# The last shared-expert step moved behind the routed experts, next to the closing layernorm

## The chip, the cores and the metric

The kernel runs on one core of a Trainium2 chip. It is one launch that computes two sequence-mixing layers and two feed-forward layers in f32. The metric is the device time of that launch in microseconds (us), taken as the median of several runs. A profile is one further execution, recorded by the hardware profiler. TensorE is called PE in its rows, VectorE DVE, ScalarE ACT, GpSimd POOL and SyncE SP. "PEld" is the weight load that goes with a matmul.

## The reference, cut to what matters

Only the last feed-forward layer and the layernorm around it are touched. Its input x has 4 sequences of 1024 rows with 256 columns each. The attention layers ahead of it are not changed.

```python
def _ffn(x, w1, w2, w3):
    return jax.nn.silu(x @ w1.T) * (x @ w3.T) @ w2.T

shared = jnp.zeros_like(xf)
for i in range(sw1.shape[0]):              # 2 shared experts, every row
    shared = shared + _ffn(xf, sw1[i], sw2[i], sw3[i])
logits = xf @ router_w.T + expert_bias     # 8 routed experts
rw, sel = jax.lax.top_k(logits, TOPK)      # each row goes to 2 of them
rw = jax.nn.softmax(rw)
...                                        # out = sum over the chosen experts of rw * _ffn
out = out + shared
x = _layernorm(x + out)                    # over the 256 columns
```

## The kernel before

Each of the three last phases is a block of its own: all engines meet at its end before the next one begins. Every f32 operand of a matmul is split into a high part in a shorter format (`fp32r`) and a low remainder, and each product is three matmuls (`PARTS`). The hidden size is 512, so one expert is `HM` = 4 hidden tiles of 128.

`phase_shared` works the two shared experts over 8 steps (`STEPS`) of 512 rows (`TOK`). A step is `NM` = 8 turns, one for each hidden tile of both experts. In turn m PE computes the two "up" products (12 matmuls of 512 columns), ACT takes `Silu` of one, DVE multiplies it by the other (`g`), ACT copies the high part (`ghi`), DVE subtracts to get the low part (`glo`), and PE adds the "down" product of turn m-2 (12 matmuls of 256 columns) into PSUM banks 6 and 7. `output(i)` on DVE adds the residual rows and SP stores the sum to the DRAM tensor `xs`. SP also reloads rows (`xr`) and fills the table `wall` with the weights of the 8 routed experts (`load_expert`). The first step also makes the router's logits, the second the routing. Then POOL scatters all rows by expert into the DRAM tensor `xg` with indirect DMAs (L1878).

`phase_experts` works 39 groups (`GROUPS`) of 256 gathered rows. The buffer `whl` has two slots that alternate: the high weights are cast out of `wall` by DVE, ACT and POOL, the low ones come by DMA from `wlo` (`up_low`, `down_low` on SP). PE runs the up products at L2384 (12 of 256 columns in a turn, four turns in a group), the transposes of the next group's rows at L2349, and the down products at L2364. ACT scales the result (`output`, L2311) and POOL adds it into `xs` by indirect DMA (`add_rows`, L2280), one group after the other. The small DMA `paid` (L2251) brings 16-byte pieces for all slots.

`phase_combine` is the closing layernorm of all 4096 rows, in 8 chunks of 512 consecutive rows: load from `xs` by SP and ACT (L2487, L2505), statistics on DVE (L2524), a chain of small operations in 16 columns that ends in the reciprocal square root (L2528 to L2536 and the helper `rsqrt`, L84 to L89), then scaling on ACT (L2501) and DVE (L2544) and the store to `out`. Statistics and chain are done for 4 chunks, then for the other 4.

The order of work on an engine is the order in which the code is written, and semaphores tie the engines together. `in_pairs` and `in_turns` run a body for pairs of steps with a hardware loop in the middle. A step touches rows c*128 to c*128+127 of each sequence, whereas a chunk of the closing layernorm is 512 consecutive rows of one sequence, so the last step's rows lie in the last quarter of every second chunk.

## Time and profile before

| | us |
|---|---|
| runs: median (lowest to highest of 3) | 1491.15 (1490.99 to 1496.67) |
| profiled execution, its own time | 1489.9 |
| profiled execution, span of the trace | 1488.3 |
| shared experts' 8 steps, from the first product to the last, by the trace | 782 to 1083 |
| routed experts' 39 groups | 1092.7 to 1444.8 |
| closing layernorm, first load to the end | 1457.7 to 1488.3 |

The span runs from the first to the last instruction. Busy shares over it are 92% for PE, 61% for DVE, 46% for ACT and 36% for POOL. In rows of the timeline the first number is the start and the second the duration, "x12" counts merged instructions, and square brackets hold the idle time of the engine just ahead and what ended it. Where rows are merged the duration runs from the first one's start to the last one's end.

### The profile page before, as it was taken

The page shows a single profiled execution, that of the slowest core. Times are in us where ns is not written, and L with a number is a line of the kernel's source. Part 1 is how long each engine was busy: PE and PEld are TensorE (multiplying, and loading weights), DVE is VectorE, ACT ScalarE, POOL GpSimd, SP SyncE. Part 2 cuts the span into 40 slices and gives each one's busy share as a digit, 9 for nine tenths or more (in the row PEclk, how much of TensorE's full clock was granted, in tenths as well). Part 3 has the DMA queues.
Part 4 walks back from the last instruction along what each step waited for, and adds up shares of the span by engine and source line. Part 5 has one row for each costly group of instructions (what it writes and reads, how often), then busy time and mean ns, then how long its engine had stood idle before and what let it go on. Part 6 is the DMA issues. An engine that isn't in the chain of part 4 may idle for free. (4 is left out here: it accounts for less than half of the span.)

```text
span 1488.3 us, 34037 instructions
## 1 busy us (share of the span) xinstructions
PE 1369.8 (92%) x12248; PEld 1189.6 (80%) x12248; DVE 906.9 (61%) x1924; ACT 687.1 (46%) x1260; POOL 540.9 (36%) x490
## 2 busy tenths in 40 slices
PE   6889999979999999999978999999979999999980
PEld 5778888867777777777757888888869999999980
DVE  4757676678687777787763364444345555555545
ACT  2446765544544544544533232222235555555543
POOL 0235554452345445445110025522014444444440
PEclk7799999979999999999998999999989999999995
DMA  6333442022213323312126014242178888888866
GB/s 237 118 130 108 145 153 85 30 86 105 86 58 127 116 67 127 120 63 99 61 69 257 19 51 149 96 149 68 54 198 237 230 238 233 233 244 235 230 144 229
DMA packets 101066, 204.00 MB, mean 137 GB/s; under 512 B 18433, under 2 KB 72577, under 8 KB 94721
## 3 DMA queue, kind: packets, MB, share of 16 engines
q1 hardware_dynamic: 75888, 144.66, 30.3%
q0 software_dynamic: 23088, 54.31, 12.8%
q10 hardware_dynamic: 2016, 4.08, 0.7%
q8 instruction: 44, 0.72, 0.2%
q14 instruction: 30, 0.24, 0.0%
HBM read 144.46 MB, written 58.55 MB: 136 GB/s over the span
## 5 line engine op out<-in xcount | busy, mean ns | idle before, releaser
L2384 PE MATMUL ps<-e_xhl,e_whl 128*128 128x256 f32 x1872 | 248.2, 282 | 5.1 <-DMA e_whl<-wlo 5.1
L2384 PEld LDWEIGHTS ps<-e_xhl,e_whl 128*128 128x128 f32 x1872 | 233.0, 189 | 5.6 <-issue 5.6
L1958 PE MATMUL ps<-s_xhl,s_whl 128*128 128x512 f32 x768 | 192.6, 400 | 6.1 <-PEq L1079 6.1
L1958 PEld LDWEIGHTS ps<-s_xhl,s_whl 128*128 128x128 f32 x768 | 143.8, 193 | 35.3 <-issue 6.3
L2280 POOL DMA_INDIRECT xs<-e_y,e_slot_id x78 | 121.8, 1561 | 83.1 <-ACT e_y L2311 68.5
L463 POOL TENSOR_TENSOR b_hhl<-b_h,b_hhl 128x512 fp32r<-128x512 f32 x64 | 94.5, 1479 | 139.6 <-ACT b_hhl L727 118.1
L2364 PE MATMUL ps<-e_whl,e_ghl 128*128 128x256 f32 x936 | 137.7, 282 | 0.5 <-DVE e_ghl L2458 0.5
L2446 DVE TENSOR_TENSOR e_g<-ps,e_act_h 128x256 f32<-128x256 f32 x156 | 66.2, 425 | 115.8 <-ACT e_act_h L2325 115.8
L2364 PEld LDWEIGHTS ps<-e_whl,e_ghl 128*128 128x128 f32 x936 | 120.5, 188 | 0.7 <-ACT e_ghl L2335 0.7
L2138 DVE TENSOR_TENSOR d_g<-ps,d_act_h 128x512 f32<-128x512 f32 x64 | 44.2, 691 | 124.4 <-PE ps L1958 87.4
L2325 ACT ACTIVATE e_act_h<-ps 128x256 f32<-128x256 f32 x156 | 60.0, 385 | 111.4 <-PE ps L2384 111.4
L560 PE MATMUL ps<-b_w,b_hhl 128*128 128x256 f32 x768 | 105.3, 287 | 6.2 <-DVE b_turned_rows L833 5.4
L560 PEld LDWEIGHTS ps<-b_w,b_hhl 128*128 128x128 f32 x768 | 99.2, 192 | 11.5 <-issue 5.8
L1937 PEld LDWEIGHTS ps<-s_whl,d_ghl 128*128 128x128 f32 x768 | 101.2, 192 | 4.8
L1937 PE MATMUL ps<-s_whl,d_ghl 128*128 128x256 f32 x768 | 104.5, 287 | 0.0
L547 PE MATMUL ps<-b_xhl,b_w 128*128 128x512 f32 x384 | 104.2, 406 | 0.1
L2273 POOL CAST e_whl<-wall 128x1024 fp32r x39 | 40.5, 1039 | 165.7 <-PE ps L2364 118.1
L1476 ACT ACTIVATE c_qf<-c_cf,fc 128x512 f32<-128x512 f32 x64 | 46.2, 722 | 117.8 <-DVE c_cf L1607 117.8
L1258 POOL TENSOR_TENSOR c_elo<-c_eraw,c_ehi 128x1024 fp32r<-128x1024 f32 x24 | 57.2, 2382 | 107.2 <-ACT c_ehi L1493 99.4
L2458 DVE TENSOR_TENSOR e_ghl<-e_g,e_ghl 128x256 fp32r<-128x256 f32 x156 | 66.1, 424 | 41.2 <-ACT e_ghl L2335 41.0
L1607 DVE TENSOR_SCALAR c_cf<-ps,fc 128x1024 f32<-128x1024 f32 x64 | 85.6, 1337 | 4.8 <-PE ps L1390 4.4
L2002 ACT ACTIVATE d_ghl<-d_g 128x512 fp32r<-128x512 f32 x64 | 40.4, 632 | 100.9 <-DVE d_g L2138 98.7
(356 smaller groups left out, 2654.4 us busy)
## 6 DMA issues: line engine op xcount, KB each, us to landing
e_whl<-wlo SPq DMA_DIRECT2D x39, 1024.0 KB, 5.1
e_whl<-wlo SPq DMA_DIRECT2D x39, 512.0 KB, 3.8
c_eraw<-in_expert_w POOLq DMA_DIRECT2D x24, 512.0 KB, 4.9
wlo<-c_elo POOLq DMA_DIRECT2D x24, 512.0 KB, 3.0
wall<-in_expert_w SPq DMA_DIRECT2D x8, 1536.0 KB, 8.5
xg<-b_zeros POOLq DMA_DIRECT2D x13, 780.0 KB, 3.8
e_xr<-xg SPq DMA_DIRECT2D x39, 260.0 KB, 3.9
x<-rows_out SPq DMA_DIRECT2D x16, 512.0 KB, 3.2
```

Source lines behind the costliest of these rows:

```text
L463: gp.tensor_tensor(hhl[:, m % 4, 1], h[:, m % 4], hhl[:, m % 4, 0].bitcast(F32), ALU.subtract).then_inc(s["hlo_ready"], 1)
L547: mm = pe.matmul(ps[:, H + m % 2, :], w1s[:, wp, kd, m * P:(m + 1) * P], xhl[:, k, xp, kd, :], start=q == 0, stop=q == 3 * KD - 1)
L560: mm = pe.matmul(ps[:, O + b // 2, lo:lo + D], hhl[:, m % 4, hp, b * P:(b + 1) * P], w2s[:, wp, m, :], start=m == 0 and q == 0 and b % 2 = ...
L1607: ve.tensor_scalar(cf[:, u % 2], ps[:, FB:FB + 2, :], fc[:, HIGH], fc[:, LOW], ALU.min, ALU.max).then_inc(s["clip_done"], 1)
L1937: mm = pe.matmul(ps[:, O + b // 2, (b % 2) * D:(b % 2 + 1) * D], ghl[:, m % 4, gp_, b * P:(b + 1) * P], whl[:, wp_, m // HM, lo:lo + D], s ...
L1958: mm = pe.matmul(ps[:, H + 2 * (m % 2) + w, :], whl[:, wp, e, lo:lo + P], xhl[:, k, xp, kd, :], start=q == 0, stop=q == 3 * KD - 1)
L2280: gp.indirect_dma_start(xs, bass.IndirectOffsetOnAxis(ap=slot_id[:, i, b:b + 1], axis=0), y[:, k, b, :], None, compute_op=ALU.add).then_in ...
L2325: act.activation(act_h[:, m], ps[:, H + m, 0:SLOT], ACT.Silu).then_inc(s["silu_done"], 1)
L2364: mm = pe.matmul(ps[:, O + k, b * D:(b + 1) * D], ghl[:, m, gp_, b * P:(b + 1) * P], whl[:, k, wp_, lo:lo + D], start=m == 0 and q == 0 an ...
L2384: mm = pe.matmul(ps[:, H + m, w * SLOT:(w + 1) * SLOT], whl[:, k, wp, lo:lo + P], xhl[:, k, xp, kd, :], start=q == 0, stop=q == 3 * KD - 1)
L2446: ve.tensor_tensor(g[:, m], ps[:, H + m, SLOT:2 * SLOT], act_h[:, m], ALU.mult).then_inc(s["g_ready"], 1)
L2458: ve.tensor_tensor(ghl[:, m, 1], g[:, m], ghl[:, m, 0].bitcast(F32), ALU.subtract).then_inc(s["glo_ready"], 1)
```

## The change

The shared phase now does 7 steps (`LAST = STEPS - 1`). Step 7's rows go into `xs` as they are (SP stores them from `xr`), so that the routed experts' additions land on them. In step 2 SP writes the split shared weights from SBUF to a new DRAM tensor `shared_hl` (6 MB in two DMAs), and waits for them before the phase ends.

In the experts' block SP loads the last step's rows (`rows7`) at the start. After the last group PE, ACT and DVE work the last shared step there (`turn7`, `up7`, `down7`, `high7`, `low7`), with the weights brought back from `shared_hl` into the two slots of `whl`. `phase_combine` is gone: its 8 chunks are loaded by SP once all scattered additions have landed, DVE makes their statistics between the turns of the last shared step (`STATS_AT`), ACT scales chunks 0, 1, 2, 4, 5 and POOL chunks 3, 6, 7. The rows of step 7 in the odd chunks are left out of the stores (96 of 128 partitions); they are finished on their own by DVE at the end, from the shared sum in PSUM plus their rows of `xs` (`x7`).

```diff
@@ phase_shared, SP
-            for i in range(STEPS):
+            for i in range(LAST):
...
+                if i == 2:
+                    for e in range(SHARED):
+                        sp.dma_start(shared_hl[:, e], whl[:, :, e].bitcast(F32)).then_inc(s["kept_out"], 16)
...
                 if i == 5:
-                    sp.wait_ge(s["xlo_ready"], STEPS)
+                    sp.wait_ge(s["xlo_ready"], LAST)
                     load_expert(5)
+            sp.wait_ge(x_in[LAST % 2], 16 * (LAST // 2 + 1))
+            sp.dma_start(xs[LAST], xr[:, LAST % 2, :, 0:D]).then_inc(s["stored"], 16)
+            sp.wait_ge(s["kept_out"], 16 * SHARED)
@@ phase_shared, PE (ACT and DVE alike)
-            in_pairs(pe, PAIR, body)
+            in_turns(pe, LAST, body)
@@ phase_experts, SP
+            sp.dma_start(rows7[:], last_x3).then_inc(f["rows7_in"], 16)
...
+            def shared_weights(n):
+                k = SLOT_OF[n]
+                sp.wait_ge(s["h_done"], HM * (GROUPS - 1 + n))
+                sp.dma_start(whl[:, k, :, 0:W2AT].bitcast(F32), shared_hl[:, n, :, 0:W2AT]).then_inc(shared_up_in[n], 16)
+                sp.wait_ge(s["g_used"], HM * (GROUPS - 1 + n))
+                sp.dma_start(whl[:, k, :, W2AT:WCOLS].bitcast(F32), shared_hl[:, n, :, W2AT:WCOLS]).then_inc(shared_down_in[n], 16)
...
+            sp.wait_ge(scattered, 16 * SB * GROUPS)
+            for i in range(STEPS):
+                sp.dma_start(x[:, bb(i)], xs_rows[i]).then_inc(rows_in[i], 16)
+            sp.dma_start(x7[:], last_xs).then_inc(f["x7_in"], 16)
@@ phase_experts, POOL, behind the last scatter
+            for i in GP_ROWS:
+                gp.wait_ge(f["scales_ready"], 1 + i // HALF)
+                for b in range(BATCH):
+                    t = i * BATCH + b
+                    last = gp.tensor_scalar(o[:, t, :], x[:, t, :], small[:, 3, t:t + 1], small[:, 5, t:t + 1], ALU.mult, ALU.add)
+                last.then_inc(f["by_gp"], 1)
@@ phase_experts, ACT
+            for m in range(NM):
...
+                act.activation(act7[:, m % 2], ps[:, H + 2 * (m % 2), :], ACT.Silu).then_inc(f["silu7_done"], 1)
...
+                act.activation(ghl7[:, m % 4, 0], g7[:, m % 2], ACT.Copy).then_inc(f["ghi7_ready"], 1)
+                if m == 0:
+                    act.wait_ge(scattered, 16 * SB * (GROUPS - 2))
+                    output(GROUPS - 1, (GROUPS - 1) % 2)
+                if m >= 6:
+                    normalise(ACT_ROWS[m - 6])
+            for i in ACT_ROWS[2:]:
+                normalise(i)
@@ phase_experts, PE
+                    if m == 1 and is_turn(j, k, GROUPS - 1):
+                        turn7()
...
+            pe.wait_ge(f["xhi7"], 1)
+            pe.wait_ge(f["xlo7"], 1)
+            for m in range(NM):
+                up7(m)
+                if m == 0:
+                    for m_ in (2, 3):
+                        down(GROUPS - 1, (GROUPS - 1) % 2, m_, (GROUPS - 1) // 2)
+                if m >= 2:
+                    down7(m - 2)
+            for m in range(NM - 2, NM):
+                down7(m)
@@ phase_experts, DVE
+            STATS_AT = {3: (0,), 4: (1, 2), 5: (3,), 6: (4, 5), 7: (6, 7)}
...
+            for m in range(NM):
...
+                ve.tensor_tensor(g7[:, m % 2], ps[:, H + 2 * (m % 2) + 1, :], act7[:, m % 2], ALU.mult).then_inc(f["g7_ready"], 1)
+                ve.wait_ge(f["ghi7_ready"], m + 1)
+                ve.tensor_tensor(ghl7[:, m % 4, 1], g7[:, m % 2], ghl7[:, m % 4, 0].bitcast(F32), ALU.subtract).then_inc(f["glo7_ready"], 1)
+                for i in STATS_AT.get(m, ()):
+                    chunk_stats(i)
+                if m == 5:
+                    scales(slice(0, HALF * BATCH))
+                if m == NM - 1:
+                    scales(slice(HALF * BATCH, TILES))
+            ve.wait_ge(f["g7_used"], NM)
+            ve.wait_ge(f["x7_in"], 16)
...
+                ve.tensor_tensor(z7[:, two], ps[:, O + half, :].rearrange("p (b d) -> p b d", b=2), x7[:, two], ALU.add).then_inc(f["z7_ready"], 1)
...
+            scales(slice(TILES, TILES + BATCH))
```

PE, before: the end of the last group of routed experts, up to the jump that ends the block. "e_whl" holds the expert's weights, "e_xhl" the split rows, "e_ghl" the split hidden values.

```order
L2364 MATMUL ps<-e_whl,e_ghl 128x256 x6
L2384 MATMUL ps<-e_xhl,e_whl 128x256 x12
L2364 MATMUL ps<-e_whl,e_ghl 128x256 x6
L2384 MATMUL ps<-e_xhl,e_whl 128x256 x12
L2364 MATMUL ps<-e_whl,e_ghl 128x256 x18
L2202 UNCONDITIONAL_BRANCH
```

PE, now: the same place. "f_xhl_10072" holds the split rows of the last shared step (`xhl7`), L2468 is `up7` and L2483 is `down7`.

```order
L2500 MATMUL ps<-e_whl,e_ghl 128x256 x6
L2468 MATMUL ps<-f_xhl_10072,e_whl 128x512 x12
L2500 MATMUL ps<-e_whl,e_ghl 128x256 x12
L2468 MATMUL ps<-f_xhl_10072,e_whl 128x512 x24
L2483 MATMUL ps<-e_whl,e_ghl 128x256 x12
L2468 MATMUL ps<-f_xhl_10072,e_whl 128x512 x12
```

The first up product of the shared step now stands ahead of the group's last two down products; four more pairs like the last two rows follow, and a last row of 36 down matmuls.

DVE, before: the end of the experts' block and the start of the closing layernorm.

```order
L2458 TENSOR_TENSOR e_ghl<-e_g,e_ghl 128x256
L2202 UNCONDITIONAL_BRANCH
L2515 UNCONDITIONAL_BRANCH
L2524 BN_STATS f_stats<-f_x 128x6 x16
L2528 TENSOR_TENSOR f_small<-f_stats 128x16
L2529 TENSOR_TENSOR f_small<-f_stats 128x16
L2530 TENSOR_TENSOR f_small<-f_stats 128x16
```

DVE, now: turns 3, 4 and 5 of the last shared step. L2657 is the product `g7`, L2659 its low part, L2628 the statistics, L2638 the start of the chain of small operations.

```order
L2657 TENSOR_TENSOR e_g<-ps,e_act_h 128x512
L2659 TENSOR_TENSOR e_ghl<-e_g,e_ghl 128x512
L2628 BN_STATS e_stats<-f_x 128x6 x4
L2657 TENSOR_TENSOR e_g<-ps,e_act_h 128x512
L2659 TENSOR_TENSOR e_ghl<-e_g,e_ghl 128x512
L2628 BN_STATS e_stats<-f_x 128x6 x8
L2657 TENSOR_TENSOR e_g<-ps,e_act_h 128x512
L2659 TENSOR_TENSOR e_ghl<-e_g,e_ghl 128x512
L2628 BN_STATS e_stats<-f_x 128x6 x4
L2638 TENSOR_TENSOR e_small<-e_stats 128x16
```

The statistics stand between the products on which PE waits, and the first chain (19 small operations) stands ahead of turn 6's product.

## Rows read from the trace of the kernel before

**Rows 1.** The page: TensorE's granted clock in 40 slices (tenths of full speed)

```profile
PEclk7799999979999999999998999999989999999995
```

**Rows 2.** Timeline of SP's queue, steps 5 and 6 of the shared experts (start, duration)

```profile
1023.18 0.37 SPq L1846 DMA_DIRECT2D xs<-rows_out  x1
...
1056.89 27.87 SPq L1846 DMA_DIRECT2D xs<-rows_out  x2
```

**Rows 3.** Timeline of POOL: its last scatter of the shared phase

```profile
1038.29 1.36 POOL L1878 DMA_INDIRECT xg<-s_xr,pos  x1 [0.30 <-issue]
```

**Rows 4.** Timeline: one turn of a shared step

```profile
1067.40 2.94 PE L1958 MATMUL ps<-s_xhl,s_whl 128*128 128x512 f32 x12
...
1070.18 1.59 PE L1937 MATMUL ps<-s_whl,d_ghl 128*128 128x256 f32 x12
1070.43 0.69 DVE L2138 TENSOR_TENSOR d_g<-ps,d_act_h 128x512 f32<-128x512 f32 x1 [2.13 <-PE ps L1958]
...
1071.83 0.69 DVE L2140 TENSOR_TENSOR d_ghl<-d_g,d_ghl 128x512 fp32r<-128x512 f32 x1 [0.70 <-ACT d_ghl L2002]
```

**Rows 5.** Timeline: the start of the routed experts

```profile
1086.74 1.04 POOL L2273 CAST e_whl<-wall 128x1024 fp32r x1 [47.08 <-issue]
1086.82 1.50 DVE L2402 CAST e_whl<-wall 128x1024 fp32r x1 [2.46 <-issue]
1087.08 0.36 SPq L2241 DMA_DIRECT2D e_whl<-wlo  x1
...
1092.72 4.45 PE L2384 MATMUL ps<-e_xhl,e_whl 128*128 128x256 f32 x24 [3.10 <-DMA e_whl<-wlo]
...
1097.01 0.60 PE L2349 MATMUL ps<-ident,e_xr 128*128 128x128 f32 x4
...
1103.84 0.36 PE L2384 MATMUL ps<-e_xhl,e_whl 128*128 128x256 f32 x1 [1.97 <-DMA e_whl<-wlo]
```

**Rows 6.** Line 2402 (DVE's cast): minimum, median, maximum in ns, first and last start

```profile
L2402 DVE CAST e_whl<-wall x39: 681/682/1498, 1086.8 to 1427.5; 128x1024 fp32r x39
```

**Rows 7.** Timeline: the last group of the routed experts

```profile
1433.95 1.58 PE L2384 MATMUL ps<-e_xhl,e_whl 128*128 128x256 f32 x12
...
1443.86 0.94 PE L2364 MATMUL ps<-e_whl,e_ghl 128*128 128x256 f32 x6 [0.54 <-DVE e_ghl L2458]
1444.88 0.84 ACT L2311 ACTIVATE e_y<-ps,e_slot_p 128x256 f32<-128x256 f32 x2 [1.62 <-DMA xs<-e_y,e_slot_id]
...
1449.19 1.54 POOL L2280 DMA_INDIRECT xs<-e_y,e_slot_id  x1 [0.30 <-issue]
```

**Rows 8.** Tile e_y from 1430 to 1460 us: its scatters from issue to landing

```profile
DMA to landing us min/median/max: 3.5/3.8/4.1
```

**Rows 9.** Timeline: the closing layernorm

```profile
1457.69 2.00 SPq L2487 DMA_DIRECT2D f_x<-xs  x4
...
1462.34 5.41 DVE L2524 BATCH_NORM_STATS2 f_stats<-f_x 128x6 f32<-128x256 f32 x16 [18.63 <-DMA f_x<-xs]
1467.79 0.18 DVE L2528 TENSOR_TENSOR f_small<-f_stats 128x16 f32<-128x16 f32 x1
...
1471.17 5.31 DVE L2524 BATCH_NORM_STATS2 f_stats<-f_x 128x6 f32<-128x256 f32 x16
1471.29 7.97 ACT L2501 ACTIVATE f_o<-f_x,f_small 128x256 f32<-128x256 f32 x16 [25.57 <-DVE f_small L2536]
...
1480.02 2.67 DVE L2544 TENSOR_SCALAR f_o<-f_x,f_small 128x256 f32<-128x256 f32 x8
...
1484.62 0.34 ACTq L2513 DMA_DIRECT2D out<-f_o  x1
```

**Rows 10.** Stretches: busy us of PE, PEld, DVE, ACT, POOL (instructions), PEclk, DMA share, GB/s

```profile
1447.00:1448.00 1.00, 0.00 (x0) 0.00 (x0) 0.00 (x0) 0.00 (x0) 0.66 (x1) 0.68 0.00 0
...
1464.00:1466.00 2.00, 0.00 (x0) 0.00 (x0) 2.00 (x7) 0.00 (x0) 0.00 (x0) 0.50 1.02 416
```

**Rows 11.** Groups of POOL by form: count, busy us, mean ns

```profile
L1279 POOL TENSOR_TENSOR s_sq<-s_qk 128x1024 f32<-128x1024 f32 x14 | 26.3, 1899 | 25.3 <-DVE s_qk L1561 25.2
```

More of the change, by code:

```diff
@@ L1766, in phase_shared @@
         PAIR = STEPS // 2
+        LAST = STEPS - 1
         ROWS = 16 * BATCH * TOPK
@@ L2168, in body @@
                             places()
-                    elif m == 5 and not zeroth and not is_turn(j, k, STEPS - 1):
+                    elif m == 5 and not zeroth and not is_turn(j, k, LAST - 1):
                         split_kept(i + 1, 1 - k, kept[:, i - 1] if isinstance(i, int) else kept[:, bass.ds(i - 1, 1)].rearrange("p i k n -> p (i k) n"))
@@ L2233, in phase_experts @@
         part = [slice(q * QC, (q + 1) * QC) for q in range(NQ)]
+        NM = SHARED * HM
+        ALL_H = HM * GROUPS
+        SLOT_OF = (GROUPS % 2, 1 - GROUPS % 2)
+        bb = lambda i: slice(i * BATCH, (i + 1) * BATCH)
+        HALF = STEPS // 2
+        ACT_ROWS, GP_ROWS = (0, 1, 2, 4, 5), (3, 6, 7)
         def expert_of(eng, i):
@@ L2337, in _, with normalise @@
             in_turns(act, GROUPS, body)
-            act.wait_ge(scattered, 16 * SB * (GROUPS - 2))
-            output(GROUPS - 1, (GROUPS - 1) % 2)
+            def normalise(i):
+                act.wait_ge(f["scales_ready"], 1 + i // HALF)
+                for b in range(BATCH):
+                    t = i * BATCH + b
+                    last = act.activation(o[:, t, :], x[:, t, :], ACT.Identity, bias=small[:, 5, t:t + 1], scale=small[:, 3, t:t + 1])
+                last.then_inc(f["by_act"], 1)
+            for m in range(NM):
+                act.wait_ge(f["h7_done"], 2 * m + 1)
+                if m < 2:
+                    act.wait_ge(s["g_ready"], ALL_H - 2 + 2 * m)
+                else:
+                    act.wait_ge(f["g7_ready"], m - 1)
+                act.activation(act7[:, m % 2], ps[:, H + 2 * (m % 2), :], ACT.Silu).then_inc(f["silu7_done"], 1)
+                act.wait_ge(f["g7_ready"], m + 1)
+                wait(act, f["g7_used"], m - 3)
+                act.activation(ghl7[:, m % 4, 0], g7[:, m % 2], ACT.Copy).then_inc(f["ghi7_ready"], 1)
[6 more added lines that the diff above has]
+                normalise(i)
         @block.tensor
@@ L2395, in _ @@
             in_turns(pe, GROUPS, body)
-            for m in (2, 3):
-                down(GROUPS - 1, (GROUPS - 1) % 2, m, (GROUPS - 1) // 2)
+            pe.wait_ge(f["xhi7"], 1)
+            pe.wait_ge(f["xlo7"], 1)
+            for m in range(NM):
+                up7(m)
+                if m == 0:
+                    for m_ in (2, 3):
[4 more added lines that the diff above has]
+                down7(m)
         @block.vector
@@ L2456, in body @@
                         slots()
+                    if m == 2 and last:
+                        high7()
+                    if m == 3 and last:
+                        low7()
                     ve.wait_ge(s["ghi_ready"], n + 1)
@@ new lines, in _ @@
+            ve.wait_ge(f["g7_used"], NM)
+            ve.wait_ge(f["x7_in"], 16)
+            for half in range(2):
+                two = slice(2 * half, 2 * half + 2)
+                ve.tensor_tensor(z7[:, two], ps[:, O + half, :].rearrange("p (b d) -> p b d", b=2), x7[:, two], ALU.add).then_inc(f["z7_ready"], 1)
+            for b in range(BATCH):
+                ve.wait_ge(f["z7_ready"], b // 2 + 1)
+                row_stats(TILES + b, z7[:, b, :])
+            scales(slice(TILES, TILES + BATCH))
@@ L2548, in build_program @@
+            ve.wait_ge(f["scales_ready"], 3)
+            for b in range(BATCH):
+                t = TILES + b
+                last = ve.tensor_scalar(o7[:, b, :], z7[:, b, :], small[:, 3, t:t + 1], small[:, 5, t:t + 1], ALU.mult, ALU.add)
+            last.then_inc(f["by_dve"], 1)
 def build_program(nc, A, out):
```

201 lines of the change are left out of this document (119 added, 82 removed).

## The prediction

> **What bounds the kernel now.** I read the page's slices first: TensorE is at 90% or more nearly everywhere, at full clock but for a few slices [rows 1], and the last slice is the only one in which it does nothing. So two things can give time: fewer matmuls ahead of 1444.8, or work for the 43.5 us that follow. Then I read the timeline at four places. In the shared phase a step takes 33.7 us, the distance of two stores to `xs` (1023.18 to 1056.89) [rows 2]. Each turn there is 4.2 us of matmuls back to back, 2.6 up and 1.6 down, with DVE's two operations in their shadow: the product starts 3.0 us after the turn's first matmul, and the low part ends 2.1 us after that start [rows 4]. The routed experts are bound by TensorE too; it waits for weights only twice, at 1092.72 and at 1103.84 (2.0 us) [rows 5]. From 1444.8 the work is a chain with no matmul in it: last scatter, block end, loads, statistics, small operations, scaling, store [rows 7, 9].
>
> **What is removed.** Step 7 leaves the shared phase. It is 8 turns of TensorE at full clock, and everything behind moves forward by its 33.7 us, if TensorE was the last to finish. It was: POOL's last scatter ends at 1039.7 [rows 3], step 6's matmuls will end near 1083.0 - 33.7 = 1049.3, so 9 us of slack hide it. The added stores of the split weights (6.3 MB, issued behind step 3's rows near 923) take some 15 us at the 416 GB/s that the closing loads reach [rows 10]. They lie beside three and a half further steps of 33.7 us; the next load on SP's queue comes one step later and has room. If writes went at half that rate they would take 30 us and still be covered. Cost taken: 0. The block end ahead of the layernorm goes as well: the last scatter is issued at 1449.19 and lands 4.1 us later [rows 7, 8], yet the loads start at 1457.69 [rows 9], 4.4 us after it. Now SP waits for the scatters itself.
>
> **What is added at the start of the experts.** One more store of 512 KB (`xs[7]`) stands ahead of the first gather and the weights on SP's queue. At 416 GB/s it is 1.3 us, and 0.4 us to issue; before, the weights issued at 1087.08 let TensorE start at 1092.72 [rows 5], so the queue sets that start. I take 1.0, between 0.4 (hidden in idle queue time) and 1.7. The load of `rows7` (512 KB, 1.3 us) stands ahead of the second group's weights, for which TensorE already waits 2.0 us. Nothing hides it: 1.4. That wait of 3.4 us would be longer than the 2.5 us of idleness after which the clock had left 2.4 GHz behind the last group (TensorE ends at 1444.8, the stretch 1447 to 1448 shows 0.68) [rows 7, 10]. If it falls to 1.2 GHz for about as long again, another 1.7 goes. I leave that to the range.
>
> **What is added behind the last group.** From here I keep the times of the old trace, and shift at the end. The last group's first up product starts at 1433.95, its last down ends at 1444.8 [rows 7]. Of this, the last two downs (1.6) now come behind `up7(0)`, and eight transposes come in (1.2, as the four of a group take 0.60 [rows 5]): 1444.4. `up7(0)` also waits for DVE's two splits of 1024 columns, which at 0.69 us for 512 from PSUM [rows 4] are about 1.3 each. They sit behind turns 2 and 3 and end near 1445.3. Its weights (2.1 MB) are issued when group 37's hidden tiles are done, near 1433.4, and take 5.2 us at 416 GB/s, or some 9 us beside the scatters: landed by 1443, just in time. So `up7(0)` starts at 1445.3. Eight turns of 4.2 and a down of 1.6 would bring TensorE to 1480.6.
>
> The rows that DVE needs come from behind the last scatter. `down(38)` ends at 1449.5 now, ACT's copy (0.84) and the two scatters (the second issued 1.85 us behind the first, landing 4.1 later) end at 1456.8. The first chunk lands 3.0 to 4.6 us later (1457.69 to 1462.34 with two queues at once [rows 9]), by 1461.4, and each next one 1.3 us behind.
>
> DVE from turn 3 on, in order, with 1.35 us for a chunk's statistics (5.41 for 16, that is four chunks) and 3.4 for a chain (1467.79 to 1471.17) [rows 9], and 2.1 from a product's start to its low part's end [rows 4]: turn 3's low part ends at 1445.3 + 11.0 + 5.1 = 1461.4; chunk 0 to 1462.8; turn 4's product is due at 1463.6, to 1465.7; chunks 1 and 2 to 1468.4; turn 5 to 1470.5; chunk 3 and the first chain to 1475.3; turn 6 to 1477.4, when it was due at 1472; chunks 4, 5 to 1480.1; turn 7 to 1482.2; chunks 6, 7 to 1484.9; the second chain to 1488.3. TensorE's last down needs turn 7's low part and is done at 1483.9, so DVE sets the end and TensorE no longer does. Behind it: the sum with the rows 1.3, statistics 1.35, chain 3.4, four scalings 1.35 (2.67 for eight [rows 9]) = 1495.7, and the store 3.7 (1484.62 to the end of the span) = 1499.4. ACT's five chunks cost 2.0 each (7.97 for four [rows 9]); two come behind the second chain and end at 1492.5, hidden. POOL's scaling is not in the trace. Its 256 columns lie between 0.27 (the cast at 1.04 for 1024 [rows 5]) and 0.7 (two inputs at 1.90 for 1024 [rows 11], with a fixed part). Eight behind the second chain end between 1490.5 and 1493.9, also hidden by DVE's last 7.4 us.
>
> **DVE and POOL at the same time.** DVE's first cast took 1.50 us where the median is 0.68, and it began 0.08 us after POOL's cast of 1.04 [rows 5, 6]: it stood still until POOL was done. POOL's eight scalings will run beside DVE's last chain, so DVE can lose at most POOL's busy time there, 2.2 to 5.6 us, and nothing if its small operations don't collide. I take 2.0. The Trainium skill, SBUF — State Buffer, section "Who interferes with whom", says that the two engines lock a port pair for whole instructions, also where a DVE operation has two SBUF inputs. By that rule most of the chain's links would collide and the loss is nearer 5, as rival B has it; the one slow cast agrees with the lock, and no row here shows it for small operands.
>
> **The sum.** 1499.4 - 33.7 + 1.0 + 1.4 + 2.0 = 1470.1 of span, against 1488.3: 18.2 us less. The profiled execution took 1489.9, its span is 1.6 us shorter, and the median of the runs is 1.25 above it. 1491.15 - 18.2 = 1473.
>
> **The rivals.** A, the forecast, DVE's chain ends last: 1468 (no collision, no cost at the start, a shorter last chain) to 1477. B, the fillers come late or collide fully. If chunk 0 lands 4 us later (a scatter beside 3 MB of weight loads), each stall is in front of a product and the chain moves by about 3; the full lock adds 3, the clock at the second group 1.7, in all 1473 + 8 = 1481. For it speaks that statistics stand in program order ahead of products; against it, that the first chunk has over 1 us to spare before turn 4. C, the change doesn't do what it says: the experts' start doesn't move the full 33.7, because SP's queue (the 6.3 MB store, table loads) or the scatters end later than step 6. That needs 9 us of delay before the first microsecond shows; with 20 us it gives 1473 + 11 = 1484. D, the slower one: TensorE runs the last shared step at 1.2 GHz, since it waits for DVE in it. All 33.7 us of turns double and DVE then follows TensorE: 1445.3 + 67.4 + 3.2 for the last down, then 11.1 of closing work is 1527.0, with the shift 1495.7, as a run 1498.6 and with a collision 1500. It decides from about 26 us of half clock (18.2, and the 8 that DVE hides). Against it: its first waits are short (about 1 us ahead of `up7(0)`, none until the sixth down), and the clock fell only in slices with real gaps [rows 1].
>
> **How the numbers follow.** A 0.70, B 0.15, C 0.07, D 0.04, and 0.04 for better than 1468 (chunks and splits cheaper than taken). The predicted time is A's, 1473. The range 1468 to 1482 takes in A and B and leaves about 0.16 out. About 0.5% (7.5 us) is what a measurement of this kernel can tell from no change. Faster by more than that is below 1483.7: A, B, the better case and most of nothing else, 0.88. Within it falls C and half of D, 0.09; slower 0.03.
>
> **What would show it.** The experts' first up product near 1060 (1092.7 - 33.7 + 1), a wait of 3 to 4 us in the second group, the last group's end as before; `up7` turns 4.2 us apart with a full clock; products of turns 6 and 7 late by 3 to 6 us behind statistics and chain; the last chain of waits all on DVE, with links over 0.2 us where POOL is busy; a span near 1470. I would be wrong if the turns of the last step are longer than 4.3 us from the start (weights late, or clock), if chunk 0 lands after turn 4's product is due, or if POOL ends last.

## The result, and the profile after

The changed kernel takes 1478.24 us (median of 4 runs, 1475.18 to 1480.26), the kernel before 1491.07 (4 runs, 1488.08 to 1496.67): a ratio of 0.991, with an interval of 0.9892 to 0.9928: faster by 0.9%, more than the 0.5% that a measurement can tell from no change. That is 12.8 us less, where 18.2 were forecast; 1478.24 lies inside the range, 5 us above the point. The profiled execution of the changed kernel took 1475.18, the lowest of its four, and its span is 1473.6, 14.7 less than 1488.3. The spans of the other three are 1475.6 to 1478.7. So 3.5 us of the 5 are in the trace (1473.6 against the sum's 1470.1) and the rest is that the profiled run was a quick one: the median lies 4.6 us above its span, where 2.9 were reckoned.

The page of the changed kernel, its granted clock in 40 slices and SP's DMA queue. TensorE works into the last slice now (its last matmul ends at 1457.9, 15.8 us ahead of the end of the span), and that slice shows 8 tenths of the clock instead of 5 [rows 1]. The queue carries 161.4 MB.

```profile
PEclk9799999989999999999998999999899999999998
...
q1 hardware_dynamic: 79840, 161.44, 33.6%
```

**The start of the experts** (timeline: start, duration, engine, line, in brackets the idle time ahead and what ended it). It answers to [rows 5].

```profile
1050.26 1.29 DVE L2133 TENSOR_TENSOR rows_out<-ps,s_xr 128x512 f32<-128x512 f32 x2 [2.13 <-PE ps L1944]
1051.57 0.37 SPq L1847 DMA_DIRECT2D xs<-rows_out  x1
1051.98 0.51 SPq L1867 DMA_DIRECT2D xs<-s_xr  x1
...
1055.25 0.36 SPq L2279 DMA_DIRECT2D e_whl<-wlo  x1
...
1057.03 1.04 POOL L2341 CAST e_whl<-wall 128x1024 fp32r x1 [1.71 <-DMA xs<-s_xr]
...
1057.41 10.58 SPq L2290 DMA_DIRECT2D e_rows<-x  x1
...
1062.65 4.54 PE L2520 MATMUL ps<-e_xhl,e_whl 128*128 128x256 f32 x24 [4.36 <-DMA e_whl<-wlo]
```

TensorE's last down product of the shared phase ends at 1050.2 where it ended at 1083.0, and the first up product of the experts starts at 1062.65 where it started at 1092.72. The pause between the two was 9.7 us and is 12.4. Two rows are new: the store of `xs[7]` (L1867) and the load of `rows7` (L2290). The DMA issued behind `paid` (L2289), the one in 16-byte pieces, stands 10.58 us in the queue, and the second group's weights come behind it. In the kernel before, the DMA in that place stood 8.94 us.

**The second group.** TensorE's first matmuls of it, and the stretches around them (busy time of PE, PEld, DVE, ACT, POOL with instructions, then the granted clock, DMA share, GB/s):

```profile
1075.16 2.08 PE L2520 MATMUL ps<-e_xhl,e_whl 128*128 128x256 f32 x12 [3.30 <-DMA e_whl<-wlo]
```

```profile
1074.00:1076.00 2.00, 0.84 (x7) 0.88 (x8) 0.00 (x0) 0.00 (x0) 0.00 (x0) 1.00 1.10 427
1076.00:1078.00 2.00, 2.00 (x12) 2.00 (x12) 0.31 (x1) 0.38 (x1) 0.00 (x0) 0.54 0.85 348
1078.00:1080.00 2.00, 2.00 (x13) 2.00 (x13) 1.05 (x3) 0.42 (x1) 0.00 (x0) 0.61 0.02 8
1080.00:1082.00 2.00, 2.00 (x19) 2.00 (x19) 1.02 (x2) 1.24 (x2) 0.20 (x1) 1.00 0.00 0
```

The wait is 3.3 us long, before it was 1.97 [rows 5]. Behind it TensorE is as busy as ever, but 12 and 13 matmuls go through in 2 us where 19 do at full clock: it works at 1.2 GHz for some 3.4 us.

**The last group and the last shared step**, from the timeline. The scatters are POOL's L2348, `up7` is L2468, `down7` L2483, the chunk loads L2324, the statistics L2628, the product `g7` L2657 and its low part L2659:

```profile
1415.41 0.84 ACT L2385 ACTIVATE e_y<-ps,e_slot_p 128x256 f32<-128x256 f32 x2 [1.45 <-DMA xs<-e_y,e_slot_id]
...
1417.26 1.22 DVE L2575 TENSOR_TENSOR f_xhl<-ps,f_xhl 128x1024 fp32r<-128x1024 f32 x1
...
1418.58 2.97 PE L2468 MATMUL ps<-f_xhl,e_whl 128*128 128x512 f32 x12 [2.21 <-issue]
...
1426.99 1.54 POOL L2348 DMA_INDIRECT xs<-e_y,e_slot_id  x1 [7.08 <-DMA xs<-e_y,e_slot_id]
...
1432.73 3.88 SPq L2324 DMA_DIRECT2D f_x<-xs  x8
...
1436.25 1.41 DVE L2628 BATCH_NORM_STATS2 e_stats<-f_x 128x6 f32<-128x256 f32 x4 [1.50 <-DMA f_x<-xs]
...
1437.58 0.68 DVE L2657 TENSOR_TENSOR e_g<-ps,e_act_h 128x512 f32<-128x512 f32 x1
...
1449.08 0.69 DVE L2657 TENSOR_TENSOR e_g<-ps,e_act_h 128x512 f32<-128x512 f32 x1
...
1450.46 0.98 DVE L2659 TENSOR_TENSOR e_ghl<-e_g,e_ghl 128x512 fp32r<-128x512 f32 x1 [0.70 <-ACT e_ghl L2429]
...
1456.19 1.66 PE L2483 MATMUL ps<-e_whl,e_ghl 128*128 128x256 f32 x12 [2.94 <-DVE e_ghl L2659]
```

The turns are 4.15 us apart. Turn 6's product starts at 1449.08, directly behind the first chain, and TensorE waits for its last down product 2.94 us, for DVE's low part. From there on DVE alone is late. Its last stretch, with POOL's scaling (L2370) beside it:

```profile
1462.09 1.28 DVE L2670 TENSOR_TENSOR rows_out<-ps,f_x 128x512 f32<-128x512 f32 x2
1462.21 4.04 ACT L2417 ACTIVATE f_o<-f_x,e_small 128x256 f32<-128x256 f32 x8 [2.95 <-DVE e_small L2646]
1462.27 4.30 POOL L2370 TENSOR_SCALAR f_o<-f_x,e_small 128x256 f32<-128x256 f32 x8 [10.40 <-DVE e_small L2646]
1463.29 1.39 DVE L2628 BATCH_NORM_STATS2 e_stats<-rows_out 128x6 f32<-128x256 f32 x4
1464.72 0.26 DVE L2638 TENSOR_TENSOR e_small<-e_stats 128x4 f32<-128x4 f32 x1
...
1466.08 0.52 DVE L84 TENSOR_SCALAR e_smalli<-e_small 128x4 int32<-128x4 int32 x1
1466.63 0.17 DVE L85 TENSOR_SCALAR e_small<-e_smalli 128x4 int32<-128x4 int32 x1
...
1468.80 1.38 DVE L2678 TENSOR_SCALAR f_o<-rows_out,e_small 128x256 f32<-128x256 f32 x4
1470.21 0.39 SPq L2333 DMA_DIRECT2D out<-f_o  x1
```

While POOL scales (1462.3 to 1466.6) three of DVE's small operations take 0.34 to 0.52 us and one 0.26; once POOL is done each takes 0.16. POOL's scalings take 0.55 each.

**Where 1473.6 comes from.** The sum of the prediction, term by term, from the two traces:

| term | forecast, us | measured, us |
|---|---|---|
| step 7 leaves the shared phase (last down 1083.0 to 1050.2) | -33.7 | -33.7, and +0.9 because everything ahead of the experts ran 0.9 later in this execution (step 5's store 1023.18 to 1024.07) |
| last down to the experts' first up product (9.7 to 12.4) | +1.0 | +2.75 |
| second group's wait (first to second group 11.12 to 12.51) | +1.4 | +1.4 |
| clock behind that wait | 0, 1.7 in the range | +1.6 |
| last group's first up product to `up7(0)` | 11.35 | 11.74 (+0.4) |
| `up7(0)` to the end of the span | 56.1 | 55.0 (-1.1) |
| span | 1470.1 | 1473.6 |

The deviations add up: 0.9 + 1.75 + 1.6 + 0.4 - 1.1 = 3.55.

### The profile page after: what moved, and what is told of

Same layout as the page of the kernel before. It is cut to its first block and busy times, and to the rows that moved or that the text cites. A ratio compares the mean times of both kernels' runs of the same rounds, so it can differ in the third digit from the quotient of the medians.

```text
span 1473.6 us, 33922 instructions
## 1 busy us (share of the span) xinstructions
PE 1373.9 (93%) x12256; PEld 1193.2 (81%) x12256; DVE 910.9 (62%) x1943; ACT 684.1 (46%) x1256; POOL 547.9 (37%) x502
## 5 line engine op out<-in xcount | busy, mean ns | idle before, releaser
L1965 PE MATMUL ps<-s_xhl,s_whl 128*128 128x512 f32 x672 | 168.9, 401 | 6.1 <-PEq L1079 6.1
L2348 POOL DMA_INDIRECT xs<-e_y,e_slot_id x78 | 121.7, 1561 | 92.2 <-ACT e_y L2385 73.2
L1965 PEld LDWEIGHTS ps<-s_xhl,s_whl 128*128 128x128 f32 x672 | 126.1, 193 | 31.8 <-issue 6.3
L2145 DVE TENSOR_TENSOR d_g<-ps,d_act_h 128x512 f32<-128x512 f32 x56 | 38.7, 692 | 111.0 <-PE ps L1965 71.4
L2622 DVE TENSOR_TENSOR e_ghl<-e_g,e_ghl 128x256 fp32r<-128x256 f32 x156 | 66.1, 424 | 43.6 <-ACT e_ghl L2409 43.4
L1944 PEld LDWEIGHTS ps<-s_whl,d_ghl 128*128 128x128 f32 x672 | 88.8, 193 | 4.1
L1944 PE MATMUL ps<-s_whl,d_ghl 128*128 128x256 f32 x672 | 91.8, 287 | 0.0
L2409 ACT ACTIVATE e_ghl<-e_g 128x256 fp32r<-128x256 f32 x156 | 64.6, 414 | 45.8 <-DVE e_g L2606 45.8
```

Source lines behind the costliest of these rows:

```text
L1944: mm = pe.matmul(ps[:, O + b // 2, (b % 2) * D:(b % 2 + 1) * D], ghl[:, m % 4, gp_, b * P:(b + 1) * P], whl[:, wp_, m // HM, lo:lo + D], s ...
L1965: mm = pe.matmul(ps[:, H + 2 * (m % 2) + w, :], whl[:, wp, e, lo:lo + P], xhl[:, k, xp, kd, :], start=q == 0, stop=q == 3 * KD - 1)
L2348: gp.indirect_dma_start(xs, bass.IndirectOffsetOnAxis(ap=slot_id[:, i, b:b + 1], axis=0), y[:, k, b, :], None, compute_op=ALU.add).then_in ...
L2409: act.activation(ghl[:, m, 0], g[:, m], ACT.Copy).then_inc(s["ghi_ready"], 1)
L2622: ve.tensor_tensor(ghl[:, m, 1], g[:, m], ghl[:, m, 0].bitcast(F32), ALU.subtract).then_inc(s["glo_ready"], 1)
```

## The experiments

Twelve kernels ran, on two chips on which the kernel before takes 1506 to 1507 us, about 15 more than above: split_first, best2, no_pool_scaling and one_weight_load on the second, all others on the first, where the changed kernel takes 1493. So ratios are to the kernel before on the same chip, and most readings go by stretches of one trace of each kernel: **S**, from the start of the last up matmul of the shared phase to the experts' first; **G**, from there to `up7(0)`; **T**, from there to the end of the span. In the changed kernel's first trace S is 17.0, G 356.0 and T 55.0.

| run | what it is | median, us (runs) | ratio [interval] | S | G | T |
|---|---|---|---|---|---|---|
| again | the changed kernel | 1492.8 (6) | 0.9898 [0.9874, 0.9923] | 17.2 | 358.3 | 55.5 |
| store_early | `xs[7]` stored earlier | 1490.97 (6) | 0.9883 [0.9854, 0.9911] | 13.8 | 357.6 | 55.8 |
| rows_late | `rows7` loaded late | 1487.66 (5) | 0.9854 [0.9826, 0.9881] | 17.4 | 351.8 | 55.0 |
| both | those two | 1491.28 (6) | 0.9881 [0.9851, 0.9911] | 13.9 | 352.5 | 55.8 |
| before_again | the kernel before | 1506.99 (1) | | 14.3 | | |
| ln_behind | layernorm not side by side | 1500.56 (10) | 0.9961 [0.9942, 0.998] | 15.0 | 359.1 | 61.7 |
| fill_gaps | statistics in DVE's gaps | 1491.25 (6) | 0.9907 [0.9892, 0.9922] | 17.4 | 357.6 | 53.4 |
| best | both + fill_gaps | 1485.09 (6) | 0.987 [0.9847, 0.9893] | 13.8 | 352.5 | 53.5 |
| split_first | DVE's splits side by side | 1495.85 (4) | 0.9918 [0.989, 0.9946] | 17.3 | 354.0 | 57.0 |
| best2 | best + split_first | 1485.62 (4) | 0.9855 [0.9831, 0.988] | 14.0 | 350.8 | 53.9 |
| no_pool_scaling | POOL scales nothing | 1487.9 (1) | | 17.5 | 356.1 | 55.3 |
| one_weight_load | one load of shared weights | 1494.99 (1) | | 17.4 | 356.8 | 55.9 |

**The changed kernel again.**

> The changed kernel once more, so that the next three can be set against it on the same chip. Its first look had a span of 1473.6 us and its runs spread from 1475 to 1480. Theory: the spread is small shifts in the same places (the front layers' start, the clock in the second group of experts), so the first up product of the experts begins 12.4 us behind the last shared down product and the second group waits 3.3 us again. Rival: the look was a lucky one, and the usual run has another wait of 3 us in the last shared step.

The ratio agrees with the first one's. S and T repeat within 0.5 us, and the rival's further wait in the last shared step isn't there. The wait at the second group doesn't repeat: it is 4.8 us this time, not 3.3, and the half clock behind it lasts longer (the row reads 2.90 us for 12 matmuls that take 1.58 at full clock), so G is 2.3 more:

```profile
1091.31 2.90 PE L2520 MATMUL ps<-e_xhl,e_whl 128*128 128x256 f32 x12 [4.81 <-DMA e_whl<-wlo]
```

**The store of `xs[7]`, one step earlier.**

```diff
@@ phase_shared, SP
+                    sp.wait_ge(x_in[LAST % 2], 16 * (LAST // 2 + 1))
+                    sp.dma_start(xs[LAST], xr[:, LAST % 2, :, 0:D]).then_inc(s["stored"], 16)
...
-            sp.wait_ge(x_in[LAST % 2], 16 * (LAST // 2 + 1))
-            sp.dma_start(xs[LAST], xr[:, LAST % 2, :, 0:D]).then_inc(s["stored"], 16)
```

> SP stores the last step's rows (xs[7]) one step earlier, behind the table load of step 5, and not between the last store and the first gather. Theory: this 512 KB store in the queue is why the experts start 12.4 us behind the last shared product, where it was 9.7 before. Expected: 9.7 to 10.1 us and the whole 2 to 2.7 us faster than the changed kernel. Rival: the start is held by something else that came with the change (the wait for the stored weights, POOL's cast behind its wait for the stores): 12 us again and no gain.

Timeline of store_early, the last output of the shared phase and the start of the experts:

```profile
1067.72 1.29 DVE L2133 TENSOR_TENSOR rows_out<-ps,s_xr 128x512 f32<-128x512 f32 x2 [2.13 <-PE ps L1944]
1069.03 0.37 SPq L1847 DMA_DIRECT2D xs<-rows_out  x1
...
1071.78 0.36 SPq L2279 DMA_DIRECT2D e_whl<-wlo  x1
...
1076.85 4.56 PE L2520 MATMUL ps<-e_xhl,e_whl 128*128 128x256 f32 x24 [2.65 <-DMA e_whl<-wlo]
```

S falls by 3.4 us, to less than the 14.3 of the kernel before. From the output's start the weights are issued after 4.06 us, against 4.99 in the changed kernel, and TensorE starts 5.07 us behind that issue, against 7.40. So the store costs 0.9 us ahead of the weights' issue and 2.3 while they land. The transfer alone, 1.3 us by the prediction, is the smaller part. The 2.3 don't come every time: of the eight traces with the store at the end seven have S between 17.0 and 17.5, but ln_behind, with the same code up to here, has 15.0 (5.3 us from the weights' issue to TensorE) and waits 5.6 us at the second group instead. The four traces with the early store have 13.8 to 14.0. The whole time moves by 1.8 us, which the intervals don't separate from nothing.

**`rows7` loaded behind the weights of a late group.**

```diff
@@ phase_experts, SP
-            sp.dma_start(rows7[:], last_x3).then_inc(f["rows7_in"], 16)
...
+                if is_turn(j, k, GROUPS - 3):
+                    sp.dma_start(rows7[:], last_x3).then_inc(f["rows7_in"], 16)
```

> The load of the last step's rows (512 KB) is issued in group 36 of the experts instead of ahead of the second group's weights. Theory: it makes the second group wait 3.3 us instead of 2.0, and that longer idleness drops TensorE to 1.2 GHz for 3.4 us, which costs 1.6 more. Expected: a wait of 2.0 us at the second group, no fall of the clock behind it, 2.5 to 3 us faster than the changed kernel. Rival: the wait is set by the 16-byte pieces ahead in the queue alone, and the load only queues behind them: 3.3 us again, no gain.

TensorE's first matmuls of the second group in rows_late, and the stretches behind:

```profile
1093.88 1.66 PE L2521 MATMUL ps<-e_xhl,e_whl 128*128 128x256 f32 x12 [1.00 <-DMA e_whl<-wlo]
```

```profile
1094.00:1096.00 2.00, 2.00 (x18) 2.00 (x19) 0.49 (x3) 0.38 (x1) 0.00 (x0) 1.00 1.08 420
1096.00:1098.00 2.00, 2.00 (x20) 2.00 (x19) 1.35 (x3) 0.72 (x2) 0.00 (x0) 1.00 0.71 295
```

The wait is 1.0 us and the clock stays up. From the first to the second group it is 10.18 us, 2.3 less than the 12.51 of the first trace and 3.8 less than the 13.94 of the run again; the rest of G's 4.2 and 6.5 us goes with the clock. So the load that was priced at 1.4 costs 2.3 to 3.8 us by itself and 4 to 6.5 with the half clock behind the wait that it lengthens. The median is 5.1 us below the run again, where 2.5 to 3 were expected. The 1.0 us that is left lies behind `paid`: the weights, now next behind it, stand 10.19 us in the queue. What moving `paid` would give was not tried.

**Both at once.**

> Both edits together. Theory: the two costs lie one behind the other on SP's queue and add up: 4.5 to 5.5 us faster than the changed kernel. Rival: the second group's wait takes up what the earlier start wins, since the pieces ahead of its weights take their time either way: then about 3 us.

S 13.9 and G 352.5 show both gains, 9.1 us together, but the median is only 1.5 below the run again. The traced execution, at 1497.8 the slowest of its six (1485.2 to 1497.8), was 5 us slower than that of the run again, and its trace says where: the shared phase, in which only one DMA issue differs, took 10.9 us longer (from its first to its last up matmul 295.4 us against 284.5). That this is also what holds the median up is not shown. It leads to the next run.

**The kernel before on the same chip.**

> The kernel before, once more with a profile. On the chip of the last comparison both kernels were 15 us slower than in their first runs, and the changed kernel's trace had gaps in TensorE's stream in the shared experts' step 2 with nothing in the profile that ends them. Theory: these gaps belong to the chip and to code both kernels have, so here they are either in both kernels' traces or in neither. Rival: the change brings them (the longer straight-line code, the 6 MB store): then only the changed kernel's traces have them.

The page's group of the down products of the shared phase (count, busy us, mean ns, idle time ahead), in the changed kernel on the first chip, and in the run again:

```profile
L1944 PE MATMUL ps<-s_whl,d_ghl 128*128 128x256 f32 x672 | 91.8, 287 | 0.0
```

```profile
L1944 PE MATMUL ps<-s_whl,d_ghl 128*128 128x256 f32 x672 | 94.9, 290 | 5.9 <-issue 5.7
```

Stretches of before_again, in step 2 while POOL scatters rows into `xg`:

```profile
905.00:910.00 5.00, 1.85 (x7) 1.73 (x7) 0.54 (x1) 0.60 (x1) 3.81 (x6) 0.57 0.24 87
910.00:915.00 5.00, 2.06 (x6) 1.29 (x5) 0.85 (x2) 0.63 (x1) 4.02 (x4) 0.50 0.29 102
```

TensorE is busy for 3.9 of these 10 us; its pauses end with "issue", and its clock is near 1.2 GHz. The same gaps stand in every experiment's page (5 to 10 us ahead of L1944 alone) and in neither of the first two traces. From its first to its last up matmul the shared phase takes 320.6 us here against 304.4 in the first trace of the kernel before, and 284.5 against 270.7 in the changed kernel: 16.2 and 13.8 us of the 15. So they belong to the chip and to code that both kernels share, and their size varies from run to run, which makes medians separate less here. What makes the gaps stays open; nothing in the trace ends them.

**The layernorm behind the step instead of beside it.** The statistics of all chunks come behind turn 7, and ACT scales nothing before.

```diff
@@ phase_experts
-            STATS_AT = {3: (0,), 4: (1, 2), 5: (3,), 6: (4, 5), 7: (6, 7)}
+            STATS_AT = {7: (0, 1, 2, 3)}
...
-                if m == 5:
-                    scales(slice(0, HALF * BATCH))
                 if m == NM - 1:
+                    scales(slice(0, HALF * BATCH))
+                    for i in range(HALF, STEPS):
+                        chunk_stats(i)
                     scales(slice(HALF * BATCH, TILES))
...
-                if m >= 6:
-                    normalise(ACT_ROWS[m - 6])
-            for i in ACT_ROWS[2:]:
+            for i in ACT_ROWS:
                 normalise(i)
```

> The last shared step stays behind the experts, but the statistics and chains of the 8 chunks all stand behind its turn 7 and no longer between the turns; ACT scales its chunks behind its last turn. Theory (DVE sets the end): turn 7's low part ends 34 us behind the first product of the last shared step, then 10.8 us of statistics, two chains of 3.4 and the closing work of 11.7 follow: the stretch from that first product to the end grows from 55.0 to 63.5 us, the kernel is 8 to 9 us slower than the changed one. Rival (TensorE's turns set the end and the filling costs about as much as it saves): under 3 us slower, the turns being shorter.

T is 61.7, 6.2 more than in the run again, where 8.5 more than 55.0 were expected; 1.2 of the difference is that turn 7's low part ended 32.8 us behind `up7(0)` and not 34. The medians are 7.8 apart. So the placement side by side is worth 6 to 8 us. Without it the moved step, with the block end that goes with it, is a gain of 0.39% [0.2%, 0.58%].

**Statistics in DVE's gaps.** DVE waits 0.70 us for ACT's high part ahead of every low part. Two of a turn's statistics go in there.

```diff
@@ phase_experts, DVE
+                mine = [t for i in STATS_AT.get(m, ()) for t in range(i * BATCH, (i + 1) * BATCH)]
+                ahead_ = 2 if m > 3 else 0
+                for t in mine[:ahead_]:
+                    ve.wait_ge(rows_in[t // BATCH], 16)
+                    row_stats(t, x[:, t, :])
                 ve.wait_ge(f["ghi7_ready"], m + 1)
...
-                for i in STATS_AT.get(m, ()):
-                    chunk_stats(i)
+                for t in mine[ahead_:]:
+                    ve.wait_ge(rows_in[t // BATCH], 16)
+                    row_stats(t, x[:, t, :])
```

> In turns 4 to 7 two of the statistics move ahead of the low part, into the 0.7 us in which DVE waits for ACT's copy of the high part. Theory (DVE sets the end): it fills four such waits, and the stretch from the first product of the last shared step to the end is 2.5 to 2.8 us shorter than 55.0. Rival (the arrival of the chunks or TensorE sets the end): no change over 0.5 us.

```profile
1465.63 0.69 DVE L2657 TENSOR_TENSOR e_g<-ps,e_act_h 128x512 f32<-128x512 f32 x1
1466.24 0.74 DVE L2628 BATCH_NORM_STATS2 e_stats<-f_x 128x6 f32<-128x256 f32 x2
1467.03 0.99 DVE L2664 TENSOR_TENSOR e_ghl<-e_g,e_ghl 128x512 fp32r<-128x512 f32 x1
```

The timeline of fill_gaps shows the low part close behind the statistics, with no idle time of its own (its 0.99 us are shown to be POOL's doing by the run without POOL's scaling). T is 53.4, 2.1 less than in the run again, although TensorE ran its first turn at a granted clock of 0.50 to 0.66 there (1436 to 1440). Against store_early and both, with the same slow first turn (T 55.8), it is 2.4 less. The median is 1.5 us below the run again, which the intervals don't separate.

**All three together.**

> The two earlier edits on SP's queue (the store of xs[7] one step earlier, the load of the last step's rows in group 36) and the filled waits. Theory: 3.3 us at the start of the experts (17.1 to 13.8 from the last shared up product to the first of the experts), 4 to 6 behind it (356 to 358 down to 352 from there to the first product of the last shared step), 2.6 in the tail: together 9 to 11 us faster than the changed kernel, 1.4 to 1.6% faster than the kernel before. Rival: the gains at the start are taken back by later waits for the last step's weights: 3 to 5 us.

S 13.8, G 352.5, T 53.5: each gain is there, and the median is 7.7 us below the changed kernel on the same chip (1485.09 against 1492.8), where 9 to 11 were expected. It is 1.3% faster than the kernel before, its interval 1.07% to 1.53%. The runs don't tell it from rows_late alone (1.46%); the traces do, by 4.4 us in S, G and T together.

**The two splits of step 7's rows side by side.** `low7()` moves from turn 3 to directly behind `high7()` in turn 2.

```diff
@@ phase_experts, DVE
                     if m == 2 and last:
                         high7()
-                    if m == 3 and last:
                         low7()
```

> In the last group DVE makes the low part of the last step's rows (1.2 us) directly behind their high part in turn 2, ahead of the group's own low part and next product. In the changed kernel TensorE waits 2.2 us ahead of the first product of the last shared step, and in half of the traces its clock falls there. Theory: that wait is DVE's order (the low part stands behind two operations that ACT delays while it waits for a scatter to land), so the wait shrinks from 2.2 to 0.6 us and the stretch from the first up product of the experts to the first product of the last shared step by 1.5 us; with the clock that stays up, 1.5 to 3 us faster. Rival: the wait is for the weights coming back from DRAM, then it stays at 2 us.

TensorE's wait ahead of `up7(0)`, and the first chunk's statistics, in the timeline of split_first:

```profile
1439.02 3.01 PE L2468 MATMUL ps<-f_xhl,e_whl 128*128 128x512 f32 x12 [0.55 <-issue]
...
1458.68 1.40 DVE L2627 BATCH_NORM_STATS2 e_stats<-f_x 128x6 f32<-128x256 f32 x4 [3.45 <-DMA f_x<-xs]
```

The wait shrinks from 2.21 us (1.93 in the run again) to 0.55, so it was DVE's order and not the weights. T grows from 55.5 to 57.0: DVE now waits 3.45 us for the first chunk where it waited 1.97 in the run again. TensorE's gain is given back to the chunks, which come when the scatters are done, 19.7 us behind `up7(0)` instead of 18.2. The ratio, 0.9918, shows no gain.

> All four edits: the early store, the late load of the last step's rows, the filled waits, and the low part directly behind the high part. Theory: 1.5 us off the best so far in the last group, and the clock does not fall in the first turn of the last shared step: 10 to 13 us faster than the changed kernel, 1.4 to 1.8% faster than the kernel before. Rival: the chunks' arrival sets the tail once the turns come earlier, and the new gain is below 1 us.

On top of the others it makes G 1.7 less and T 0.4 more, and the clock stayed up in the first turn as expected. The runs show none of it: 1485.62 us and a ratio of 0.9855 on the second chip, 1485.09 and 0.987 for best on the first, with intervals that overlap. The 10 to 13 us that were expected didn't come.

**No scaling on POOL.** The three chunks 3, 6 and 7 are stored as they were loaded, so that this kernel does less.

```diff
@@ phase_experts, SP
+                src = x if i in GP_ROWS else o
...
@@ phase_experts, POOL
-                for b in range(BATCH):
-                    t = i * BATCH + b
-                    last = gp.tensor_scalar(o[:, t, :], x[:, t, :], small[:, 3, t:t + 1], small[:, 5, t:t + 1], ALU.mult, ALU.add)
-                last.then_inc(f["by_gp"], 1)
+                gp.sem_inc(f["by_gp"], 1)
```

> POOL's twelve scalings are left out (chunks 3, 6 and 7 are stored unscaled). Theory (DVE stands still while POOL holds the shared port): the last chain of 19 small operations in 4 columns, 4.05 us from its first to its last start and end in the changed kernel with single operations of 0.26 to 0.52, takes 3.3 with every operation at 0.15 to 0.17; the low part of turn 6 takes 0.69 and not 0.98. So the collision costs 0.7 us in the last chain, 1.0 in all. Rival: the long operations come from something else (semaphores of the stores, the fetch of the code): they stay.

Its last chain in the timeline, the first and the last operation, and the one that took 0.52 us:

```profile
1477.60 0.17 DVE L2636 TENSOR_TENSOR e_small<-e_stats 128x4 f32<-128x4 f32 x1
...
1478.49 0.17 DVE L84 TENSOR_SCALAR e_smalli<-e_small 128x4 int32<-128x4 int32 x1
...
1480.66 0.16 DVE L2644 TENSOR_TENSOR e_small<-e_small 128x4 f32<-128x4 f32 x1
```

From 1477.60 to 1480.82 the chain takes 3.2 us, against 4.05 beside POOL (1464.72 to 1468.77). The collision costs 0.8 us there and 0.3 in turn 6's low part (0.98 us, here 0.69), together 1.1. T is 55.3 all the same, 0.3 less than in the run again: the first chunk came 0.2 later, and from the issue of the last store to the end it is 4.0 us instead of 3.4.

**One load of shared weights instead of two.** The second shared expert works with the first one's weights, so that 3 MB less move while the scatters are under way.

```diff
@@ phase_experts
-        SLOT_OF = (GROUPS % 2, 1 - GROUPS % 2)
+        SLOT_OF = (GROUPS % 2, GROUPS % 2)
...
@@ phase_experts, SP
-            for n in range(SHARED):
-                shared_weights(n)
+            shared_weights(0)
...
```

> The second shared expert's weights (3 MB) aren't loaded; its turns use the first one's. Theory: the two scatters of group 37 need 8.5 us to land and hold up the last ones and with them the chunks, because 2 + 1 + 2 MB of weights stand in the same 16 DMA engines; without the second load they land 1.5 to 2.5 us sooner, the last scatter starts within 7.0 us of the first product of the last shared step instead of 8.4, and DVE no longer waits for chunk 0 (1.5 us in the changed kernel). Rival: the first load alone makes them late, or the scatters themselves do: the same 8.4 us.

Landing times of the scatters of the last three groups (tile `e_y`), first in the run again, then here:

```profile
DMA to landing us min/median/max: 3.6/7.9/8.9
```

```profile
DMA to landing us min/median/max: 3.6/3.8/9.2
```

The median goes from 7.9 to 3.8 us, which is that of the kernel before [rows 8]. The last pair of scatters is issued 7.2 us behind `up7(0)` instead of 8.7, the chunk loads 12.8 instead of 14.7, and the first statistics wait for nothing. That last part says little: TensorE ran its first turn at 1.2 GHz in this run (granted clock 0.63 and 0.52 from 1438 to 1442), its turns were 1.6 us late, and with equally late turns and both loads the wait was only 0.3 to 0.4 us (store_early, both, fill_gaps). T is 55.9. One scatter still took 9.2 us, beside the first load. The cause of the late chunks is shown by the landing times and the earlier issues, in one trace; what it is worth at the end is not.

## Why the prediction was right

**The frame held.** The shared phase gave back the 33.7 us of one step; the 9 us of slack behind the scatters and the 6.3 MB store in step 2 hid what they were to hide. The store's two parts landed in 13.8 to 22.3 us and nothing waited for them. Rival C, a start that doesn't move, is out. TensorE's turns in the last step are 4.15 us apart at full clock, products 4 and 5 come 0.8 and 1.2 us late, product 6 is 4.0 late behind the first chain, and DVE's low part releases the last down product. DVE's chain ends last, which is rival A. The second chain ends 43.6 us behind `up7(0)`, forecast 43.0. Rival D didn't come; where the clock fell in the first turn (store_early, both, fill_gaps, best and one_weight_load, 5 of the 12 traces), it was for 3 to 4 us, far from the 26 that D needs.

**Mis-sized: the store ahead of the experts.** The step "I take 1.0, between 0.4 and 1.7" counted a transfer at full rate and an issue. It measured 2.75, outside its bounds; the run with the early store shows 3.4 for the same store on another chip. It delays the issue of the weights by 1 us and their landing by 2 more; the step had 0.4 for the first and the bare bytes, 1.3, for the second, and took less than the two together.

**Mis-sized: the second group.** The 1.4 for the load came as 1.4, but that is luck: it is the distance to the kernel before. The run with the late load, where only the load is gone, puts it at 2.3 us against the first trace, so 0.9 us of it was hidden. The queue's rows show where: from the issue of `paid` to the second group's first product it was 15.4 us and is 18.5 now (1088.49 to 1103.84, 1056.65 to 1075.16), 3.2 more, but TensorE starts its first group 6.0 us behind that issue where it was 4.2, because of the store's delay, and waits 1.8 less for that. The step "Nothing hides it: 1.4" counted bytes and an issue, as with the store. The 1.7 for the clock, which was left to the range, came as 1.6, and belonged in the sum: the text itself had a row with a clock already down after 2.5 us of idleness, and forecast 3.4 us of waiting. rows_late puts the two together at 4.2 us against the first trace's G and at 6.5 against the run again.

**Mis-sized the other way: the closing chain.** 2.0 us for the collision measured 1.1, DVE's last chain without collision is 3.2, not 3.4, and the last store ends 0.3 earlier. From the sum with the rows (1462.09) to the end it is 11.5 us, where 13.1 were in the sum. The rule of the Trainium skill that stood beside this (SBUF — State Buffer, "Who interferes with whom": DVE and POOL lock a shared port for whole instructions) would, by the prediction's estimate, have cost nearly 5. The trace shows a stretch of 0.18 to 0.35 us on each of three small operations and of 0.1 on a fourth, and one of 0.3 on a larger one; the other four links beside POOL go through at their usual length. So the direction agrees and the price worked out from the rule doesn't.

**Half right: the first chunk.** It was to land 16.1 us behind `up7(0)`, just as DVE was ready for it, and over 1 us ahead of turn 4's product. It came 17.7 behind it, and DVE waited 1.5 us for it: this is the mechanism of rival B, scatters that take 8 us beside the shared weights' loads, as one_weight_load shows. By the rows it cost 0.8 us: turn 4's product was due 4.15 behind turn 3's (1432.67), at 1436.82, and came at 1437.58, and from the first statistics on DVE has no other pauses than those for ACT's high part.

**Small: `up7(0)`.** It was to wait about 1 us and waited 2.2. ACT stood 1.45 us in front of a scatter's landing, its high part for DVE came late, and `low7` with it; split_first takes this away, and the chunks take the gain back.

## What to carry to other kernels

A small transfer put ahead of a stage's first weights costs more than its bytes: it delays the next loads, and TensorE's wait for them may have half clock behind it (3.4 to 6.9 us of it behind waits of 3.30 and 4.81 here). Put it a step earlier or many groups later, which gave 3.4 and 4 to 6.5 us in the traces; of the medians only the second one's 5.1 us stands out of the spread. And when an engine other than TensorE ends last, spend the effort on that engine's gaps and on when its inputs arrive: 2.1 us of T came from filling DVE's idle 0.7 us pieces, while of TensorE's shorter wait ahead of `up7(0)` (1.93 to 0.55 us) T took 1.5 back.

## What was not expected of the hardware

A wait of 1.97 us ahead of the second group left TensorE's clock at 2.4 GHz, and so did 1.00; waits of 3.30, 4.23 and 4.81 us were followed by 1.2 GHz, for 3.4 us in one trace and 6.9 in another. The length of the wait alone doesn't decide it: 1.83 us in split_first were followed by 1.2 GHz too (the clock had come back from the pause at the experts' start only 4.5 us before), and of the waits ahead of `up7(0)` 2.10 to 2.34 us were in five traces, while 1.93 to 2.33 were not in five others. An indirect DMA that adds 128 rows into `xs` lands in 3.8 us in the kernel before and, as a median of six, in 7.9 beside loads of 1 and 2 MB. On some chips TensorE's instruction stream has gaps of its own while POOL's scatters run (busy 11.0 of 20 us in before_again, from 900 to 920), and there both kernels took about 15 us longer; the cause of the gaps is open.
